# Block-sparse attention with a SwiGLU layer on Trainium2: key and value tiles moved by one block of 64 against the query tiles

## The reference

```
def attend(qx, kx, vx):
    scores = jnp.einsum('bhqd,bhkd->bhqk', qx, kx) * scale
    return jnp.einsum('bhqk,bhkd->bhqd', jax.nn.softmax(scores, axis=-1), vx)
first_ctx = attend(qb[:, :, 0], k, v)                  # block 63 likewise
exp_k = jnp.concatenate([kb[:, :, 1:-3], kb[:, :, 2:-2], kb[:, :, 3:-1]], axis=3)
inner = jnp.einsum('bhlqd,bhlkd->bhlqk', qb[:, :, 2:-2], exp_k) * scale
band = jnp.concatenate([first_band, inner, last_band], axis=-1)
aw = jax.nn.softmax(band, axis=-1)                     # then aw @ the same blocks of v
...
x = x + _layernorm(attention(_layernorm(x)))           # Wq, Wk, Wv with biases
x = x + _layernorm(ffn(_layernorm(x)))                 # silu(x @ wg.T) * (x @ wu.T) @ wd.T, hidden 3072
```

## Time and profile before

| Stage (core 1) | from, us | to, us |
|---|---|---|
| prologue, to the first scores | 0 | 71.9 |
| 64 slots of attention | 71.9 | 521.0 |
| feed-forward layer | 521.0 | 1523.0 |

### The profile page before, as it was taken

The page is one execution under the profiler, slowest core; times in us unless marked ns, Lnnn a source line. Parts: engine busy times, 40 slices in busy tenths (PEclk is TensorE's granted clock), DMA queues, the critical chain, the costliest instruction groups (busy, mean ns, idle before and its releaser), DMA issues.

```text
span 1523.0 us, 27094 instructions; the slowest of 8 cores (1519.3 to 1523.0 us)
## 1 busy us (share of the span) xinstructions
PE 1495.9 (98%) x10136; PEld 732.0 (48%) x10136; DVE 663.0 (44%) x1247; ACT 467.5 (31%) x610; POOL 255.1 (17%) x566
## 2 busy tenths in 40 slices
PE   5999999999999999999999999999999999999998
PEld 4455555555555544444444444444444444444444
DVE  5364454565634355254244344334525424533113
ACT  5475555555556611021011111111101111111111
POOL 2022232333323431010010010010001001000001
PEclk9999999999999999999999999999999999999999
DMA  7745677878855988232323322423322333312002
GB/s 245 253 116 109 132 147 162 165 157 171 144 122 113 301 269 230 75 94 77 108 98 98 88 100 75 105 95 100 104 77 86 88 103 104 97 49 97 0 1 97
DMA packets 131488, 184.75 MB, mean 121 GB/s; under 512 B 65696, under 2 KB 97440, under 8 KB 130208
## 3 DMA queue, kind: packets, MB, share of 16 engines
q1 hardware_dynamic: 114512, 112.22, 28.2%
q0 software_dynamic: 16560, 70.79, 17.1%
q10 hardware_dynamic: 288, 0.01, 0.0%
HBM read 136.85 MB, written 69.21 MB: 135 GB/s over the span
## 4 chain that ended last, share of the span: by engine, by line
PE 98%; DVE 1%; DMA 1%; issue 0%; ACT 0%; POOL 0%; DVEq 0%; SPq 0%; ACTq 0%; POOLq 0%
PE ps L752 22%; PE ps L767 22%; PE ps L823 21%; PE ps L306 14%; PE ps L352 8%; PE ps L405 5%; PE ps L463 3%; PE ps L459 1%; PE ps L466 1%; PE ps L326 1%; PE ps L710 1%; DMA xst<-x_in 1%; POOL small L175 0%; ACT xT L278 0%; DVE small L170 0%
## 5 line engine op out<-in xcount | busy, mean ns | idle before, releaser
L752 PE MATMUL ps<-x2T,wg_sb 128*128 128x512 bf16 x1536 | 362.7, 379 | 0.0
L767 PE MATMUL ps<-x2T,wu_sb 128*128 128x512 bf16 x1536 | 362.5, 379 | 0.0
L823 PE MATMUL ps<-wd_sb,hsw 128*128 128x512 bf16 x1488 | 322.5, 379 | 0.0
L759 ACT ACTIVATE sgb<-ps 128x512 bf16<-128x512 f32 x192 | 114.5, 597 | 509.4 <-PE ps L752 492.6
L773 DVE TENSOR_TENSOR hsw<-ps,sgb 128x512 bf16<-128x512 f32 x192 | 132.6, 691 | 306.0 <-PE ps L767 305.9
L767 PEld LDWEIGHTS ps<-x2T,wu_sb 128*128 128x128 bf16 x1536 | 150.2, 98 | 181.3 <-issue 0.3
L752 PEld LDWEIGHTS ps<-x2T,wg_sb 128*128 128x128 bf16 x1536 | 150.2, 98 | 180.9 <-issue 0.2
L823 PEld LDWEIGHTS ps<-wd_sb,hsw 128*128 128x128 bf16 x1488 | 145.6, 98 | 175.6
L175 POOL TENSOR_TENSOR small<-small 128x1 f32<-128x1 f32 x127 | 74.3, 585 | 773.4 <-DVE small L173 773.4
L419 ACT ACTIVATE pb<-ps 128x1024 bf16<-128x1024 f32 (+2 forms) x128 | 117.4, 956 | 124.9 <-PE ps L405 124.9
L410 ACT ACTIVATE pb<-ps 128x1024 bf16<-128x1024 f32 x128 | 124.1, 1021 | 47.0 <-PE ps L405 47.0
(11 more groups left out here) (84 smaller groups left out, 1121.0 us busy)
## 6 DMA issues: line engine op xcount, KB each, us to landing
xx<-x_in SPq DMA_DIRECT2D x34, 512.0 KB, 5.6
attn<-attn_d SPq DMA_DIRECT2D x32, 512.0 KB, 3.9
x_d<-xx POOLq DMA_DIRECT2D x32, 512.0 KB, 6.7
x1r<-x_d SPq DMA_DIRECT2D x31, 512.0 KB, 3.2
out<-x1r POOLq DMA_DIRECT2D x31, 512.0 KB, 3.0
xst<-x_in SPq DMA_DIRECT2D x29, 512.0 KB, 6.2
attn_d<-ast SPq DMA_DIRECT2D x58, 256.0 KB, 4.4
wgb_d<-wgT POOLq DMA_DIRECT2D x24, 256.0 KB, 5.3
```

Source lines behind the costliest of these rows:

```text
L752: mm = te.matmul(gp[:, p2], wg_sb[:, hc * 1024 + dc * 128:hc * 1024 + (dc + 1) * 128], xTn[:, dc * 512:(dc + 1) * 512], start=(dc == 0), s ...
L759: tok["sg", g] = AC.sig(ac.activation(sgb[:, p2], gp[:, p2], AF.Silu, scale=DQ))
L767: mm = te.matmul(upp[:, p2], wu_sb[:, hc * 1024 + dc * 128:hc * 1024 + (dc + 1) * 128], xTn[:, dc * 512:(dc + 1) * 512], start=(dc == 0), ...
L823: mm = te.matmul(ys[:, half * 512:(half + 1) * 512], hsw[:, hc * 512 + tt * 128:hc * 512 + (tt + 1) * 128], wd_sb[:, hc * DM + half * 512: ...
```

## The change

Query tiles, the tokens that are loaded and the order of chunks and slots stay. Key and value tiles other than tile 0 now begin 64 tokens earlier: tile t holds tokens 128t-64 to 128t+63. The four blocks that a query tile j needs are then exactly the tiles j and j+1, and there is a tile 32, the last block together with the first one. What follows from it in the code:

- `pv` has two band tiles for each query tile. The global queries meet tiles 4c+1 to 4c+4.
- The scores are regrouped. Unit 3: two pieces of 256 columns. Unit 2: one of 256, two of 128. Unit 0: key tiles 4c+1 to 4c+4. They are now made in the order 1, 3 and, later in the slot, 0, 2. No zeros are written ahead; a unit's exponential is one instruction. The masks of a band unit are two memsets (three for unit 2 of chunk 7).
- A value tile whose tokens lie in two chunks is put together by `x_cross`, two VectorE copies into `xTc`, once for each chunk and once for tile 32. `v_group` has two groups more (slots 6 and 7 of chunk 6).
- `kt` is laid out by `u`, with 64 columns behind the three chunks, which ScalarE fills again in chunks 3 and 6; one VectorE copy (`k0`) puts the first block behind chunk 7.

```diff
-BAND = [(2, 0, 0, 1, 1, 4), (2, 1, 0, 3, 5, 3), (2, 1, 3, -1, 0, 1),
-        (3, 0, 0, 2, 3, 4), (3, 1, 0, 4, 7, 1), (3, 1, 1, 0, 0, 3)]
-BW = 21 * 64
-PW = 2 * (512 + 512 + BW)
+PW = 4 * 1024
+KW = 3 * 512 + 64
+WHERE = {(0, 0): (2, 384), (0, 1): (2, 0), (1, 1): (2, 128), (1, 2): (3, 0),
+         (2, 2): (3, 128), (2, 3): (3, 256), (3, 3): (3, 384), (3, 4): (2, 256)}
...
+        if c in (3, 6):
+            ac.activation(kt[:, u * KW + 1536:(u + 1) * KW], bank[:, 0:64], AF.Identity,
+                          bias=bk[:, u:u + 1], scale=1.0)
...
+    def x_cross(c):
+
+        DV.need(tok["xT", 4 * c - 1], tok.get(("xT", 4 * c)), tok.get("vx"))
+        out = xTc[:].rearrange("p (d k) -> p d k", d=8)
+        dv.tensor_copy(out[:, :, 0:64], xTs[(c - 1) % 3][:].rearrange(
+            "p (d k) -> p d k", d=8)[:, :, 448:512])
+        first = xTs[c % 3] if c < NCH else xT0
+        tok["xTc", c] = DV.sig(dv.tensor_copy(out[:, :, 64:128], first[:].rearrange(
+            "p (d k) -> p d k", d=8)[:, :, 0:64]))
...
-        TE.need(tok["wv", n], tok["xT", t])
+        if j or t == 0:
+            TE.need(tok["wv", n], tok.get(("xT", t - 1)), tok["xT", t])
+        else:
+            TE.need(tok["xTc", c])
...
-        if i == 3 and c + 1 < NCH:
+        if i in (0, 2):
             TE.need(tok["k", c + 1, u])
...
-            pieces = [(g * 256 + b * 64, 4 * c + k, q[:, qf * 64:(qf + n) * 64], n * 64)
-                      for unit, g, b, k, qf, n in BAND if unit == i and 0 < 4 * c + k < NT]
+        elif i == 2:
+            pieces = [(0, 4 * c + 1, q[:, 0:256]), (256, 4 * c + 4, q[:, 384:512]),
+                      (384, 4 * c, q[:, 0:128])]
+        else:
+            pieces = [(0, 4 * c + 2, q[:, 128:384]), (256, 4 * c + 3, q[:, 256:512])]
...
-                keys = [k for k in (j - 1, j, j + 1) if 0 < 4 * c + k < NT]
...
-                for k in keys:
-                    w = WHERE[j, k]
-                    mm = te.matmul(o, p_band(c, u)[:, h, w:w + 128], v_tile(4 * c + k, u, h),
-                                   start=False, stop=(k == keys[-1]))
+                for k in (j, j + 1):
+                    unit, w = WHERE[j, k]
+                    mm = te.matmul(o, p_unit(c, u, unit)[:, h, w:w + 128],
+                                   v_tile(4 * c + k, u, h), start=False, stop=(k == j + 1))
...
+        if u == 0 and more:
+            x_cross(c + 1)
+        if (c, u) == (NCH - 2, 6):
+            x_cross(NCH)
-        scores(c, u, 0, 0)
-        scores(c, u, 1, 1)
+        scores(c, u, 1, 0)
+        scores(c, u, 3, 1)
...
         if not few:
-            scores(c, u, 2, 0)
-            scores(c, u, 3, 1)
+            scores(c, u, 0, 0)
+            scores(c, u, 2, 1)
...
+        if c == NCH - 2 and u >= 6:
+            v_group(NCH, 0, u - 6)
```

More of the change, by code:

```diff
@@ L125, in build_nc @@
     kg = at("kg", MID + 47104, 1024, BF16)
-    kt = at("kt", KV, 3 * 4096, BF16)
-    v_sb = at("v_sb", KV + 24576, 11 * VW, BF16)
+    kt = at("kt", KV, NU * KW, BF16)
+    v_sb = at("v_sb", KV + 2 * NU * KW, 11 * VW, BF16)
     pb = at("pb", PQ, 2 * PW, BF16)
     qb = at("qb", PQ + 4 * PW, 2 * 512, BF16)
+    xT0 = at("xT0", PQ + 4 * PW + 2048, 8 * 64, BF16)
+    xTc = at("xTc", PQ + 4 * PW + 3072, 8 * 128, BF16)
     wst = at("wst", TOP, 4 * 1024, F32)
@@ L408, in scores @@
         AC.need(t_s)
+        lo = pieces[0][0]
+        hi = pieces[-1][0] + pieces[-1][2].shape[1]
+        s_free[buf] = tok["p", c, u, i] = AC.sig(ac.activation(
+            p_unit(c, u, i)[:, :, lo:hi],
+            sp.rearrange("p (h e) -> p h e", h=2)[:, :, lo:hi], AF.Exp))
         if i < 2:
-            s_free[buf] = tok["p", c, u, i] = AC.sig(ac.activation(
-                p_unit(c, u, i), sp.rearrange("p (h e) -> p h e", h=2), AF.Exp))
             return
[L413 to L417, removed]
-                ac.activation(pg[:, :, 0, a:b], sg[:, :, 0, a:b], AF.Exp)
-        s_free[buf] = tok["p", c, u, i] = AC.sig(ac.activation(
-            pg[:, :, :, lo:hi], sg[:, :, :, lo:hi], AF.Exp))
-        for row, col in ((64, 0), (0, 192)):
-            PO.need(tok["p", c, u, i], (PO.sem, PO.n))
-            tok["m", c, u] = PO.sig(po.memset(pg[row:row + 64, :, :, col:col + 64], 0.0))
+        up, down = 64, 0
+        masks = [(up, 0, 64), (down, 192, 64), (up, 256, 64), (down, 448, 64)]
+        if i == 2:
+            if c == 0:
+                masks = [(down, 128, 128), masks[2]]
+            elif c == NCH - 1:
+                masks[2] = (up, 256, 128)
+        pg = p_unit(c, u, i)
+        done = []
+        for m in masks:
+            row, col, w = m
+            pair = (row, col + 256, w)
+            if m in done:
+                continue
+            PO.need(tok["p", c, u, i], (PO.sem, PO.n))
+            if pair in masks:
+                done.append(pair)
+                out = pg[row:row + 64].rearrange("p h (g e) -> p h g e", g=2)[:, :, :, col:col + w]
+            else:
+                out = pg[row:row + 64, :, col:col + w]
+            tok["m", c, u] = PO.sig(po.memset(out, 0.0))
             PO.need(tok["m", c, u])
@@ L448, in pv @@
     def pv(c, u):
-        TE.need(tok.get("ctx"), tok["p", c, u, 1], tok["m", c, u])
-        TE.need(*(tok["v", t, u // 4] for t in range(max(4 * c - 1, 0), min(4 * c + 5, NT))),
+        TE.need(tok.get("ctx"), tok["p", c, u, 2], tok["m", c, u])
+        TE.need(*(tok["v", t, u // 4] for t in range(max(4 * c, 1), 4 * c + 5)),
                 tok["v", 0, u // 4])
@@ L602, in build_nc @@
         wq_load(u)
+    DV.need(tok["xT", 0])
+    dv.tensor_copy(xT0[:].rearrange("p (d k) -> p d k", d=8),
+                   xTs[0][:].rearrange("p (d k) -> p d k", d=8)[:, :, 0:64])
     DV.need(t_small)
@@ L626, in build_nc @@
         more = c + 1 < NCH
-        scores(c, u, 0, 0)
-        scores(c, u, 1, 1)
+        if (c, u) == (NCH - 2, 0):
+            DV.need(tok["s", 5, 7])
+            tok["k0"] = DV.sig(dv.tensor_copy(
+                kt[:].rearrange("p (u e) -> p u e", e=KW)[:, :, 1024:1088],
+                kg[:].rearrange("p (u e) -> p u e", e=128)[:, :, 0:64]))
+            for v in range(NU):
+                tok["k", NCH, v] = tok["k0"]
+        if u == 0 and more:
[4 more added lines that the diff above has]
+        scores(c, u, 3, 1)
         if more and c > 0:
@@ L633, in build_nc @@
         if few and c:
-            q_group(*slots[n + 1], lambda: scores(c, u, 2, 0))
-            scores(c, u, 3, 1)
+            q_group(*slots[n + 1], lambda: scores(c, u, 0, 0))
+            scores(c, u, 2, 1)
         elif n + 1 < len(slots):
```

47 lines of the change are left out of this document (22 added, 25 removed).

## The result

| | runs | median, us | lowest | profiled execution |
|---|---|---|---|---|
| before | 9 | 1531.05 | 1528.84 | 1524.09 |
| after | 9 | 1520.58 | 1518.31 | 1518.31 |

The ratio of after to before is 0.9941, 95% interval 0.9921 to 0.9960: 9.0 us less, between 6.1 and 12.1. The medians differ by 10.5. (Executions far above the rest, such as one of 1638.86 us, count in this table but not in the ratios, nor in any time behind this table; without them the medians are 1530.11 and 1520.12.)

A forecast was written before the change was run, and what follows sets the result against it. TensorE, busy 98% of the span, was taken to bound the kernel. Fewer `pv` matmuls (-13.9 us) and two more value groups (+3.4) gave -10.5, all else 0: 1531.05 to 1520.6 us, range 1517.5 to 1525.

The forecast's parts named there:

- step 1: `pv` blocks of the attention: 464 matmuls fewer at 0.030 us each, all on the path, 13.9 us less.
- The rival that the weight load sets the pace: Each removed `pv` matmul takes its 98 ns weight load with it: 45 us less 3.4, 1489 us; chance 0.01.
- step 2: Slots 6 and 7 of chunk 6: two more value groups at 1.72 us each, 3.4 us more.
- step 3: Regrouped scores in the attention slots: same columns and borders, taken as 0, bounds 2.8 us less to 3.2 more.
- steps 4 and 5: TensorE's waits for exponentials and, in `v_group`, on the semaphore from `xTc`: taken as 0, the latter up to 1.6 us.
- The tightest hand-over: Second score unit of the next slot waiting for a band exponential: 0.16 us left, so no wait.
- step 6: Added VectorE copies (at most 0.75 us each), ScalarE activations, GpSimd memset and weight DMAs: covered, off TensorE's path.
- The sign that was to show an error: In the profile after, TensorE was to have no new wait above 0.1 us.
- The sum: Whole kernel: 13.9 us less and 3.4 more make 10.5 us less, profiled execution from 1524.09 to 1513.6.
- The time forecast: Median of the runs: 1531.05 less 10.5 gives 1520.6 us, keeping the 7 us above the profiled execution; chance 0.90.

The follow-up runs named there:

- experiment 2: Kernel before with only the last two band tiles of each query tile multiplied with the values, 464 `pv` matmuls left out: 1516.35 us, ratio 0.9922 to before.
- experiment 4: Kernel before with its scores made in the order 1, 2 and later 0, 3, nothing else changed: 1527.71 us, ratio 0.9996 to before.
- experiment 8: Changed kernel with 6 of the 72 feed-forward weight conversions, all loads taken from those 6: 1513.87 us, ratio 0.9901 to before.
- the second ratio: Changed kernel measured once more without an edit, on the second chip: 1519.38 us, ratio 0.9934 to before.
- experiment 3: Changed kernel without the two value groups of tile 32: 1516.05 us, ratio 0.9912 to before.
- experiment 9: Kernel before with 6 of the 72 weight conversions, all feed-forward loads taken from those, on the third chip: 1526.21 us, ratio 0.9972 to before.

## Why the prediction was right

*Price of a `pv` matmul, step 1.* Right. 0.030 us each by what a `pv` block has lost in the profile after (8 matmuls, 1.07 us for 1.31), 14.1 us for 464 in experiment 2, 13.9 predicted. The rival that the weight load sets the pace is out. The Trainium skill, "TensorE: Matmul & The Clock Gate", section "Back-to-back issue gap", states 81 ns for a matmul of 128 columns in a stream of weight loads and matmuls; these have 65 columns and a load of 128 for each, and 30 ns. The N/2.4 + 2.5 ns that the section gives for a matmul by itself, 29.6 ns here, held in the stream.

*Value groups, step 2.* Right: 3.5 us by the attention alone, 3.2 to 3.8 by the quartiles, 3.4 predicted.

*Scores, step 3.* Right at 0: 0.55 and 0.54 us for the two blocks, and experiment 4 for another regrouping, -0.3 us in the quartile.

*Waits, steps 4 and 5.* Right. The tightest hand-over kept 0.17 us, for 0.16 predicted, and the value group behind `xTc` starts without a gap, so a wait on a new semaphore that is already over cost nothing there.

*Beside the path, step 6.* The copies took 0.29 us each, for a bound of 0.75. But this step says of DMAs only that the weights' have no new wait. It doesn't look at the transposes of the tokens, whose room between issue and use is two slots and so shrinks with the slot. Most of what the slowest core loses comes from there (5.5 us in experiment 8). The trace of before has no such wait on any core, and one execution was taken for all. The sign that was to show an error, no new wait of TensorE above 0.1 us, is not kept on five cores of the profile after (0.3 to 3.9 us); as the kernel before has such waits too, the sum was not touched.

*The sum.* 10.5 us predicted; 10.7 on a core without a late transpose (1521.2 to 1510.5, same chip), 10.1 by the first measurement's quartile, 10.3 with the conversions gone, and 10.4 in the attention alone (449.1 to 438.7, and 449.0 to 438.6 with the conversions gone). The feed-forward layer kept its length, as forecast. On the slowest core of eight 9.0 (6.1 to 12.1) and 10.1 (by the second ratio, 0.9934). The time forecast, 1520.6, was met at 1520.58, and here luck has a part. The 7 us from the profiled execution to the median carried over because both kernels have late transposes, which the prediction didn't know. And the agreement within 0.1 us is closer than the medians are themselves: by the medians of 1530.11 and 1520.12 the difference is 10.0, and the ratio's 9.0 has an interval of 6 us.

Whether some of the gain comes back through them: of the cores of before, on the first two chips, 80 of 408 stood 4 us above their quartile, of the changed kernel 37 of 96, and of the one in experiment 2, with equally short slots, 13 of 40. Two slots are 14.9 us now where they were 15.4. That may cost about 1 us, an estimate from the 9.0 and 10.1 us by the ratios against 10.5. It is counted over cores of few runs and not shown by a run that changes only the room; experiment 3, as short, had 8 of 40.

## What to carry to other kernels

Price a run of small matmuls by the distance between the starts of blocks, and take the border to another kind of matmul (0.09 us here) off it; the records' own lengths, 193 ns here for 30, don't add up. Where the profiled execution is faster than the median, look for what it lacks, in a second profile of the same kernel and on all cores, before reading margins from it: the slowest of eight cores is made by rare events that one profile may not have. Here a slot more of margin didn't cure a transfer whose tail is long; taking away what ran beside it did.

## What the runs showed of the hardware

- A matmul of 65 columns with a weight load of 128 columns of its own cost 30 ns in a stream of 32 to 40 such pairs (14.1 us for 464), though the record of one load is 98 ns: the loads overlap.
- A transposing DMA of one 128x1024 tile landed 5 to 8 us after its issue in the median of a core while the 72 converting DMAs ran beside it. The latest on a core was at 9.6 to 22.6 us, and up to 31.3 us with the transposes a slot earlier. The one that landed after 17.2 us had held SyncE for 11 us; on the cores with landings after 30.2 and 31.3 us no transpose of the tokens held it for more than 5. Without the conversions the maximum over eight cores was 7.4 us, with plain copies 10.1 us.
- What a wait costs TensorE is not its length alone. Waits of 3.9 and 2.0 us cost 5.6 and 3.8, with a granted clock of 0.72 over the next 6 us and a group of eight 512-column matmuls at 2.8 to 2.9 us for 1.74. A wait of 3.6 us on another core cost 3.6, with the clock at 1.00.
- On the third chip, cores 0 to 3 had stretches with a granted clock of 0.81, while core 4 kept 1.00. In the median these cores were 3.6 us slower in the kernel before (1526.4 for 1522.8). In the profile of experiment 9 the loss was not in the attention, which took 449.0 us there as elsewhere.
